# Both maxima and both exponents of a pair of heads made in a row, in a gated cross-attention and mixture-of-experts kernel

## The reference

```python
xn = layer_norm(x, gamma_x, beta_x); ln = layer_norm(latents, gamma_l, beta_l)
q = (ln @ Wq).reshape(b, m, h, d)
kv_x = xn @ Wkv; kv_l = ln @ Wkv          # k_x is rotated (rope)
sim = jnp.einsum('bhid,bhjd->bhij', q, k) # k, v: 375 context rows, then 112 own rows
attn = jax.nn.softmax(sim, axis=-1)
out = jnp.einsum('bhij,bhjd->bhid', attn, v)
...
x = x + jnp.tanh(g_xattn[0]) * out @ Wo
x = x + jnp.tanh(g_ffn[0]) * experts(_layernorm(x))   # top 2 of 8, gelu
```

## Time and profile before

| | |
|---|---|
| median of 3 runs | 525.76 us (525.52 to 527.16) |
| the profiled execution's own time | 523.4 us, with a span of 521.7 us |
| busy: PE, DVE, ACT, POOL | 446.3, 289.4, 295.1, 195.4 us |
| mean granted clock of TensorE | 0.928 of full |
| starts of H0 of batches 1 to 7 | 93.50, 125.20, 156.90, 188.57, 220.27, 251.72, 277.81 us |

### The profile page before, as it was taken

How to read it: one execution, slowest core, us unless ns; L and a number is a source line. 1 busy time by engine, 2 the same in 40 slices (tenths; PEclk the granted TensorE clock), 3 DMA queues, 4 the chain that set the end, 5 groups by cost and what they waited for, 6 DMA issues and landing times. The chain is left out here.

```text
span 521.7 us, 9510 instructions
## 1 busy us (share of the span) xinstructions
PE 446.3 (86%) x3237; PEld 373.2 (72%) x3237; DVE 289.4 (55%) x707; ACT 295.1 (57%) x652; POOL 195.4 (37%) x223
## 2 busy tenths in 40 slices
PE   2674699999989999899998764589999999999990
PEld 1453476766767677676776643279999999999990
DVE  3784324244451634435254823558888888888850
ACT  3534466765666666766767411056667667776730
POOL 4530163462825538164460165302222222333222
PEclk9976699999999999999999875569999999999997
DMA  7400010000000008999000021785777778775323
GB/s 190 117 29 1 1 31 0 9 24 2 29 1 24 5 0 252 226 215 319 12 2 1 1 71 44 233 254 175 212 204 212 219 223 232 224 206 132 44 29 90
DMA packets 41864, 56.04 MB, mean 107 GB/s; under 512 B 1745, under 2 KB 37153, under 8 KB 41808
## 3 DMA queue, kind: packets, MB, share of 16 engines
q1 hardware_dynamic: 36864, 49.80, 32.2%
q0 software_dynamic: 4960, 5.72, 7.1%
HBM read 40.37 MB, written 16.07 MB: 108 GB/s over the span
## 5 line engine op out<-in xcount | busy, mean ns | idle before, releaser
L1367 POOL DMA_INDIRECT acc_scratch<-yv,xt x28 | 49.2, 1757 | 130.6 <-DVE yv L1520 126.3
L1389 ACT ACTIVATE hf<-ph,b1t 128x256 f32<-128x256 f32 x112 | 47.0, 471 | 48.4 <-PE ph L1595 47.8
L871 DVE TENSOR_REDUCE negmax<-sc 112x1 f32<-112x487 f32 x64 | 42.2, 660 | 46.4 <-PE sc L1103 46.4
L691 ACT ACTIVATE prob<-sc,negmax 112x487 f32<-112x487 f32 x64 | 43.5, 680 | 12.6 <-DVE negmax L871 9.4
L1128 PEld LDWEIGHTS po<-probt,vals 125*64 125x64 f32 (+1 forms) x512 | 25.4, 139 | 23.5 <-issue 15.6
L699 ACT COPY probt<-pt 125x448 f32<-125x448 f32 x64 | 34.7, 542 | 11.1 <-PE pt L1111 10.9
L1103 PE MATMUL sc<-keys,queries 64*112 64x488 f32 x128 | 35.3, 629 | 6.1 <-ACT keys L640 3.4
L1502 DVE TENSOR_TENSOR hl<-hf,hh 128x512 fp32r<-128x512 f32 x56 | 38.8, 693 | 1.9
L1111 PEld LDWEIGHTS pt<-ident,prob 112*125 112x125 f32 x256 | 36.6, 191 | 4.2
L1111 PE MATMUL pt<-ident,prob 112*125 112x112 f32 x256 | 38.3, 274 | 0.0
L1500 DVE CAST hh<-hf 128x512 fp32r<-128x512 f32 x56 | 24.2, 433 | 23.7 <-ACT hf L1389 23.2
(11 more groups left out here) (273 smaller groups left out, 1372.1 us busy)
## 6 DMA issues: line engine op xcount, KB each, us to landing
w_next<-in_L_ffn_W SPq DMA_DIRECT2D x10, 1024.0 KB
rows_scratch<-blank SPq DMA_DIRECT2D x2, 4257.0 KB, 33.4
w_third<-in_L_ffn_W SPq DMA_DIRECT2D x8, 1024.0 KB
w1s<-in_L_ffn_W SPq DMA_DIRECT2D x5, 1024.0 KB
w2s<-in_L_ffn_W SPq DMA_DIRECT2D x5, 1024.0 KB, 8.7
xt<-rows_scratch SPq DMA_DIRECT2D x14, 258.0 KB, 2.8
ctx_t<-in_ctx SPq DMA_DIRECT2D x8, 375.0 KB
w1s<-in_L_xattn_Wkv SPq DMA_DIRECT2D x1, 1024.0 KB, 12.3
```

The source lines that it names most:

```text
L691: act.activation(prob[:, h % 2, 0:JA], sc[h % 2][0:M, 0:JA], ACT.Exp, bias=negmax[:, h % 2:h % 2 + 1], accum_out=total[:, p, h:h + 1]).the ...
L871: dve.tensor_reduce(negmax[:, h % 2:h % 2 + 1], sc[h % 2][0:M, 0:JA], AX, ALU.max, negate=True).then_inc(max_done.sem, 1)
L1367: pool.indirect_dma_start(out=acc_dram, out_offset=bass.IndirectOffsetOnAxis(ap=xt[i % 3][:, n, D + 1:D + 2].bitcast(I32), axis=0), in_=yv ...
L1389: last = act.activation(hf[:, n % 3, u], ph[n % 3][:, u * T:(u + 1) * T], ACT.Gelu, bias=b1t[:, col])
```

## The change

Four edits in `attention`; PE, POOL and SP keep their lists.

- ACT: `exponent` of heads h + 2 and h + 3 now stand together in even heads, between the two halves of `prepare_beside`. Before, `exponent(h + 2)` stood at the end of each head.
- ACT: `keep_prob` goes ahead of half 0.
- DVE: both `row_max` of a pair stand first in even heads, ahead of both halves, and both `invert` of the next pair behind the halves of odd heads.
- `SPLIT_AT` moves `high_out` and `scale_heads` 0 and 2 one head earlier, to H2 and H6.

```diff
-        SPLIT_AT = (3, 4, 7, 8)
+        SPLIT_AT = (2, 4, 6, 8)
...
             def head(t, p, h, previous, following, after):
+                keep_prob(t, p, h)
                 prepare_beside(prepare, h, 0, following, after)
-                keep_prob(t, p, h)
+                if h % 2 == 0:
+                    if h + 2 < H:
+                        exponent(t, p, h + 2)
+                        exponent(t, p, h + 3)
+                    elif following:
+                        exponent(*following, 0)
+                        exponent(*following, 1)
                 prepare_beside(prepare, h, 1, following, after)
                 late_high_out(t, p, h, previous)
-                if h + 2 < H:
-                    exponent(t, p, h + 2)
-                elif following:
-                    exponent(*following, h + 2 - H)
...
             def head(t, p, h, previous, following, after):
-                if h + 1 < H:
-                    invert(t, p, h + 1)
-                elif following:
-                    invert(*following, 0)
+                if h % 2 == 0:
+                    if h + 2 < H:
+                        row_max(t, p, h + 2)
+                        row_max(t, p, h + 3)
+                    elif following:
+                        row_max(*following, 0)
+                        row_max(*following, 1)
                 prepare_beside(prepare, h, 0, following, after)
-                if h + 2 < H:
-                    row_max(t, p, h + 2)
-                elif following:
-                    row_max(*following, h + 2 - H)
                 prepare_beside(prepare, h, 1, following, after)
+                if h % 2:
+                    if h + 1 < H:
+                        invert(t, p, h + 1)
+                        invert(t, p, h + 2)
+                    elif following:
+                        invert(*following, 0)
+                        invert(*following, 1)
```

More of the change, by code:

```diff
@@ L885, in begin @@
                 invert(t, p, 0)
+                invert(t, p, 1)
             def output(t, p, part):
```

## The result

The changed kernel takes 620.34 us (median of 6 runs, 615.84 to 623.85), against 525.73 us before: a ratio of 1.180, 95% interval 1.174 to 1.186. Forecast were 613 us, 585 to 632. The profiled execution took 615.84 us and spans 614.1 us. In the changed kernel the lines of PE, DVE and later code are numbered a little higher (transposes of probabilities L1121, scores L1113, projections L976 to L978).

A forecast was written before the change was run, and what follows sets the result against it. PE was taken to bound the attention stage, busy 30.15 of 31.67 us a batch. Added waits of 68 us at full clock plus 19 us for the clock, on a 525.8 us median, gave 613 us, range 585 to 632.

The forecast's parts named there:

- (c): H3: PE's last values wait for keep_value 2, now behind the exponent of head 5; +1.24 us a batch.
- (e): H5: the query projection waits for latl, a chain of 3.64 us against 1.74 before; +1.90 us a batch.
- (g): H7: context block 1 waits for cf, 3.21 us against 2.36 before; +0.85 us a batch.
- (f): H6: transpose_context 0 waits for the normalization, its statistics now behind two maxima; +3.08 us a batch, the largest.
- (b): H2: the last block's keys wait for low_context 2 on POOL, 3.21 us against 2.64; +0.57 us a batch.
- (d): H4: the last key transpose waits for rotate 2, 8.22 us against 6.61 with (c) counted; +1.61 us a batch.
- (a): H1: transpose_context 2 waits for keep_key 0, 3.06 us against 1.83; +1.23 us a batch.
- I take 3.2: Half clock behind the H5 and H6 waits: 3.2 us a batch, half the 6.2 bound, 19 us over six batches.
- the full-clock rival: Clock stays full throughout, so only the 68 us of waits count: 594 us; chance 0.22.
- +2: From H5 of batch 6 to the barrier: exponents save at most 2.7 us, router work loses up to 5; taken as +2.
- Waits that hide each other: Rival: waits overlap and only the two long ones, (e) and (f), count: 30 us, 556 us; chance 0.13.
- The worst case: Rival: clock falls more often, meeting 6.2 us a batch, with 5 lost at the end: 634 us or more; chance 0.07.

The follow-up runs named there:

- run 1: Kernel before with only the pairs: both exponents together on ACT, both maxima between the halves and both inverses behind odd heads on DVE; 566.29 us, ratio 1.079.
- run 2: Kernel before with only DVE's edit: both maxima of a pair first in even heads, both inverses behind the halves of odd heads; 547.30 us, ratio 1.043.
- run 11: Kernel before with exponents, maxima and inverses paired as in run 1, and four buffers prob in place of two; 526.21 us, ratio 1.000.
- run 8: Changed kernel with 16 unused identity multiplications on PE in each of the two long waits, H5 and H6 of batches 0 to 5; 608.19 us, ratio 1.157.
- run 9: Kernel before with keep_prob ahead of half 0 in every head but H2; 545.56 us, ratio 1.039.
- Run 10: Kernel before with SPLIT_AT = (2, 4, 6, 8) in batches 0 to 6 and the old (3, 4, 7, 8) in batch 7; 529.09 us, ratio 1.006.
- run 12: Kernel before with the next batch's copies lath and latl moved from H5 to behind keep_prob of head 4; 522.02 us, ratio 0.992.
- run 3: Kernel before with only keep_prob moved ahead of half 0 on ACT; 559.26 us, ratio 1.063.

## Why the prediction was right

**The mechanism and the seven terms** are shown. The chains were right within 0.08 us each, by the windows of the changed kernel; run 1 shows (c), (e) and (g) with the pairs alone, run 2 shows (f) alone, run 11 that without the wait for the buffer the pairs cost nothing. (b) and (d) have only the windows for them, and of (a) run 1 has the part without keep_prob (waits for `keys` of up to 0.6 us). Batches 1 to 5 were forecast at 52.4 us and 16 for the clock, together 68.4, and measured at 64.0. One sign did not come: the wait for `cf` was to be 1.2 us a batch and is 0.41, since half clock fills the time.

**The clock** was forecast at 19 us, half of its bound. The step that was mis-sized is "I take 3.2": it is 2.1 us a batch (12.6 us of batch growth less 10.5 of the terms), and run 8 gives the same 2.1 by another way. The bound had 3.1 us of full-clock work double behind each wait. The first stretch is over after 3.4 us, so 2.0 us of work became 3.5, 1.5 us lost; of the second most is hidden by the wait for `cf`. That such waits do bring the clock down was read rightly from the earlier trace rows, thin as it was, and the full-clock rival, 594 us, is out. By the rule of thumb of the Trainium skill (TensorE: Matmul & The Clock Gate, HAM oscillation), that only idle gaps beyond its bound matter, the clock would have stayed up. Taken as a rule on PE's idle time alone, the trace disagrees: waits of 3.07 us in the changed kernel and 2.21 in run 9 are followed by half clock. PE had run only transposes just ahead of them, though: in run 9 the last product ends at 188.40, and then come transposes and the wait until 192.42. Whether that plays a part no run here was made to show.

**Batches 6 and 7** were forecast at 4.7 + 2 and measured at 7.5 + 8.1 = 15.6. The failed step is the "+2" for what is left from H5 of batch 6 on: it was bounded by 5 and is 10 to 11. I had reckoned with exponents that come earlier, and did not go through DVE's list of batch 7. There the two maxima wait behind the router's `pick_first`, and `scale_heads` 2 stands ahead of `place`; DVE in the changed kernel:

```profile
392.37 0.27 DVE L883 TENSOR_TENSOR heads<-out_t,po 128x112 f32<-128x112 f32 x1 [3.42 <-ACT out_t L707]
392.56 0.20 DVE L147 TENSOR_TENSOR key<-pv,first 112x48 f32<-112x48 f32 x1
```

The router's last stage (L147) starts at 392.56, right behind `heads`, though PE had its sums ready at 389.03. Run 10 shows that this place of `scale_heads` 2 matters. I had no clock in this term either: in batch 7 the granted clock is 0.81 of full against 0.90 before, and 0.50 from 384.90 to 393.60, while PE makes the very values that `heads` waits for. How the 8.1 us divide between the two was not measured.

**The sum** was closer than its terms, and that is luck: in the profiled execution 7 us too much in batches 0 to 5, for the clock, stand against 9 too little at the end and 3 of the start that no term covers. The median lies 4.5 us above the profiled execution, where the forecast took 2.4. The six runs differ in the clock: the fastest, 615.84 us, had a mean granted clock of 0.888, the two slowest, 623.53 and 623.85, had 0.862. So the profiled execution shows the least of what the clock costs; for the median my estimate from run 8 is 12.2 us gained and 6 x 0.64 lost by the filler, 16.

**The rivals.** Waits that hide each other (556 us) are out, as the seven are all there. Faster needed the pair to run in a row, which ACT's timeline refutes; no effect needed room ahead of every wait, and all seven windows are longer. The worst case (634 us) did not come, though the end lost twice the 5 us it had for it: the clock did not reach its bound.

**What I would have got wrong piece by piece** is keep_prob. In the whole change its price stands inside (a), (b), (e) and (g) and is right there. By itself it costs 33 us: some 14 since it moves POOL's `rotate` 1 onto DVE's statistics (run 9), and the rest by the waits I had reckoned and the half clock behind one of them. In the whole change the same statistics are late by another reason, and start at 214.21, behind the end of `rotate` 1: one loss covers the other, which is why 10.5 us came out right without this effect in it. That too is luck: (d) takes 1.38 us for these statistics from batch 7, where no `rotate` runs beside them, and in batch 3 before they took 2.5 (170.18 to 172.66).

## What to carry to other kernels

Before putting two of a kind in a row, look at what the second waits for: if it is the engine that the queue behind it serves, everything in that queue becomes late by a round trip. As many buffers as the pair spans take that wait away, but here they gained nothing over the old order (run 11). Price such a change per wait, by the chain from the bounding engine's own step to the thing it needs, and set it against the time at which that engine came there before. The same view names the gains: what stands last in front of a wait and could be done earlier in an idle place is worth about its own length, as the two copies of run 12 are (0.56 us expected, 0.61 measured in batch 3). And when a new wait comes out of the sum, look at the clock behind it as well.

## What the runs showed of the hardware

The clock of PE falls to 1.2 GHz behind waits that are no longer than 2 to 3 us. Counted over batches 0 to 5: behind a wait of 2.2 us in four batches of six in run 9 and in five in run 3, behind one of 2.6 us in all six in run 1, behind one of 3.05 us in four in run 2, and behind 11 of the 12 waits of about 3.05 us in the changed kernel, for 3.4 us or more. So the length of the wait alone does not decide it. Unused multiplications in the waits keep the clock at 2.4 GHz and make the median 12 us lower (run 8).

Some small operations of DVE that start beside a large one of POOL last until POOL's ends: 1.25 us for one of 0.15 (run 3). The Trainium skill, Trainium Architecture — The Big Picture, section "What this means for kernel authors", says that DVE and GpSimd share a port pair with an exclusive lock; run 3 agrees, and shows three such waits in a row where there had been one. Not every DVE operation is held: in the kernel before, the maximum that starts at 169.60 us takes its usual 0.67 us wholly inside an operation of POOL that runs from 169.28 to 170.55.
